# Attention steps between single matmuls, at distances of ScalarE's work, and feed-forward products opened by weight pieces

## The chip, the cores and the metric

One Trainium2 chip, eight NeuronCores. Each core runs the same program on two of the sixteen sequences; no core waits for another. The metric is the device time of the slowest core in microseconds. Before the change it is 1290.26 us (median of three runs, 1287.92 to 1292.53). A difference of 0.3%, about 4 us, is what such runs can tell from none.

A core has TensorE (matmuls into PSUM, 8 banks of 128 x 512 fp32), VectorE, ScalarE and GpSimd, and queues that start DMAs; most DMAs here go through SyncE's.

## The reference, cut to what matters

```
x = x + 0.5 * ffn(layernorm(x))       # layer 0
x = x + attention(layernorm(x))       # layer 1: 16 heads of 64, causal, 2048 positions
x = x + 0.5 * ffn(layernorm(x))       # layer 2, same weights as layer 0

ffn(z):   s = softmax(z @ W_gate)                 # 7 columns
          w = two largest of s, scaled to sum 1
          out = z @ W_shared.T + (w1 + w2 as dispatched) * (z @ W_expert.T) + bias
attention(z): q, k, v = z @ W.T + b; softmax(q k^T / 8, causal) v; @ Wp.T + bp
```

Every token keeps both of its expert shares and all experts have one matrix, so a feed-forward layer is one product with `W_shared + W_expert` and the gate a factor per token.

## The kernel before, in words

Tokens are handled in 32 tiles of 128, four of them to a chunk, so 8 chunks, four for each sequence. Matrices lie in SBUF as bf16. A **product** (kinds `f`, `q`, `k`, `v`, `p` in the order) is eight matmuls of 128 x 512 that add up in one PSUM bank (L982, L995, L1005, L1037). VectorE then reads the bank out (L1110, L1125, L1136, L1176). There are 384 products.

Attention goes by **quads** (`qd`): 320 of them, each for two heads and two blocks of 128 keys against the 512 queries of a chunk. On TensorE a quad k is `scores(k)` (4 matmuls, L899, into banks 0 to 3) and `values(k-2)` (8 matmuls, L922, into bank 4, and 4 that sum the exponentials, L930, into bank 5). ScalarE takes the exponentials of quad k (L1273, two instructions). On a diagonal block VectorE masks (`mk`, L1161). A **unit** is all quads of two heads and one chunk: 64 units of 2, 4, 6 or 8 quads. At its end (`oe`) VectorE copies bank 4 to `OS` (L1169) and bank 5 to `DSB` (L1170); TensorE spreads the sums over the partitions with one matmul (`bc`, L1026), ScalarE takes their logarithm and its exponential (L1282, L1284), GpSimd multiplies (L757), a DMA stores (`os`).

The order of all this is one list, `ORDER`, made before the program is built; **each engine walks the same list from its start to its end and issues its own share of each entry**. So an entry that waits on an engine holds back all behind it on that engine. `a_order` gives the start, q, k, v and layer 0's feed-forward; `c_order` gives projection and layer 2's feed-forward. `make_order` walks both and puts quads in: a running sum of (quads left) / (products left) lets 0, 1 or 2 quads follow each product. Of the 384 products 262 are followed by one quad, 30 by two, 92 by none (most of these at either end). `bc` stands after the product that follows its `oe`, ahead of the next quad.

`SHARED` gives each product and each small PSUM result (`t`, `ga`, `n`, `b2`, `bc`, `bb`) a bank in turn, in the order of the list. During attention there are **two such banks, 6 and 7**:

```
    if _e == ("qd", 0):
        EARLY = list(_uses)
        _banks = (6, 7)
```

`bank_free` makes TensorE wait until the bank's last result was read out, before it writes the first matmul of a new one:

```
                b, m = SHARED[en]
                if m:
                    e.wait_ge(r_sh[b], m)
```

At the start, the 16 pieces of the two feed-forward matrices (512 KB each, fp32, half h of the outputs by quarter m of the inputs) come by SyncE's queue, and `ws` j adds a pair into `WF` (VectorE, two of them on GpSimd, L660). A product `f` of layer 0, half h waits until all four sums of that half are done.

## Time and profile before

| | us |
|---|---|
| median of the runs | 1290.26 |
| the profiled execution | 1291.16 |
| span of its slowest core (core 3) | 1289.5 |
| spans of all eight cores | 1275.2 to 1289.5 |
| TensorE busy | 1163.5 (90%) |
| VectorE busy | 755.4 (59%) |
| ScalarE busy | 741.3 (57%) |
| GpSimd busy | 437.7 (34%) |

The span runs from the first to the last instruction of a core. Busy time of TensorE is the union of the matmuls' modelled durations, so a matmul's row is longer than the distance to the next one's start; distances between starts are the better price. In an entry of the timeline the brackets hold the idle time of the engine before it and who ended that.

### The profile page before, as it was taken

To read this page: it belongs to the slowest core of one execution; us is meant where nothing else is said; L and a number is where in the kernel's file an instruction comes from. 1 tells how busy PE (TensorE), PEld (TensorE's weight loads), DVE (VectorE), ACT (ScalarE), POOL (GpSimd) and SP (SyncE) were. 2 spreads that over 40 slices of the span, in tenths; PEclk is the share of its full clock that TensorE was granted. 3 is DMA by queue.
4 is the path that set the end of the run, shared out by engine and by line. 5 is a ranking of instruction groups with operands and counts; after the bars stand their busy time and mean duration, and the time that the engine had idled before them with its cause. 6 is when DMAs were issued, how large, how long until landed. Compare 5 with 4: busy or idle time off the path is not lost.

```text
span 1289.5 us, 28541 instructions; the slowest of 8 cores (1275.2 to 1289.5 us)
## 1 busy us (share of the span) xinstructions
PE 1163.5 (90%) x9038; PEld 436.5 (34%) x9038; DVE 755.4 (59%) x1366; ACT 741.3 (57%) x936; POOL 437.7 (34%) x310
## 2 busy tenths in 40 slices
PE   3789878899999999999999999998999999898987
PEld 1334333333333333333333333332333333333343
DVE  6774797557557555445645654545756555555575
ACT  4362243377577666667666676665666666665501
POOL 3422443136035113403511523621443260515152
PEclk9899999899999999999999999999999999999999
DMA  9979645697376437424634745645574754647052
GB/s 274 314 243 272 160 114 150 171 207 203 86 187 191 103 117 215 107 90 150 190 88 126 174 127 143 198 119 155 116 221 109 235 140 151 173 142 199 14 176 82
DMA packets 209350, 207.44 MB, mean 161 GB/s; under 512 B 127283, under 2 KB 172339, under 8 KB 209206
## 3 DMA queue, kind: packets, MB, share of 16 engines
q1 hardware_dynamic: 202304, 202.42, 57.0%
q10 hardware_dynamic: 6902, 3.20, 1.0%
q8 instruction: 78, 1.28, 0.5%
q14 instruction: 66, 0.54, 0.2%
HBM read 117.49 MB, written 67.11 MB: 143 GB/s over the span
## 4 chain that ended last, share of the span: by engine, by line
PE 65%; DVE 11%; ACT 8%; issue 7%; DMA 4%; SPq 4%; DVEq 0%; POOL 0%; ACTq 0%; POOLq 0%
PE PS L995 14%; PE PS L982 12%; PE PS L922 10%; PE PS L899 9%; PE PS L1005 8%; PE PS L1037 6%; ACT PT L1273 4%; PE PS L930 4%; ACT ATT L1273 3%; DVE PT L1161 2%; SPq L787 2%; DVE BNS L1054 2%; DMA WQKV<-od 2%; DMA WQKV<-wte 1%; DVE DSB L1170 1%
## 5 line engine op out<-in xcount | busy, mean ns | idle before, releaser
L1273 ACT ACTIVATE PT<-PS,MB 128x1024 bf16<-128x1024 f32 (+3 forms) x428 | 400.8, 989 | 224.0 <-PE PS L899 221.8
L982 PE MATMUL PS<-WF,XT 128*128 128x512 bf16 x1024 | 247.8, 392 | 10.0 <-DVE WF L660 8.5
L995 PE MATMUL PS<-XT,WQKV 128*128 128x512 bf16 x1024 | 247.0, 389 | 8.3 <-ACT XT L1207 3.1
L1273 ACT ACTIVATE ATT<-PS,MB 128x1024 bf16<-128x1024 f32 x212 | 193.8, 965 | 81.5 <-PE PS L899 80.7
L750 POOL TENSOR_TENSOR SQ<-QKS 128x512 bf16<-128x512 bf16 x128 | 140.8, 1102 | 277.4 <-DVE QKS L1125 227.0
L899 PE MATMUL PS<-ATT 64*128 64x512 bf16 (+3 forms) x1280 | 187.8, 351 | 39.6 <-ACT PT L1273 26.5
L757 POOL TENSOR_TENSOR OTT<-OS,RR 128x512 bf16<-128x512 f32 x64 | 83.2, 1301 | 411.1 <-ACT RR L1284 411.0
L982 PEld LDWEIGHTS PS<-WF,XT 128*128 128x128 bf16 x1024 | 95.1, 100 | 149.3 <-issue 56.5
L995 PEld LDWEIGHTS PS<-XT,WQKV 128*128 128x128 bf16 x1024 | 93.3, 99 | 146.8 <-issue 54.7
L732 POOL TENSOR_TENSOR XC<-XC,BF 128x1024 f32<-128x1024 f32 x48 | 104.4, 2176 | 95.2 <-DVE XN L1083 95.2
L1110 DVE SCALAR_TENSOR_TENSOR XC<-PS,GG,XC 128x512 f32<-128x512 f32 x96 | 71.7, 749 | 100.1 <-PE PS L982 98.2
L922 PE MATMUL PS<-PT,ATT 128*32 128x512 bf16 (+3 forms) x1712 | 120.4, 358 | 8.3 <-DVE PT L1161 8.2
L1005 PE MATMUL PS<-WQKV,XT 128*128 128x512 bf16 x512 | 120.1, 380 | 4.1 <-DVE VST L1136 2.5
L1054 DVE BATCH_NORM_STATS2 BNS<-XC 128x6 f32<-128x512 f32 x156 | 104.5, 688 | 17.4 <-DMA XC<-x 8.3
L899 PEld LDWEIGHTS PS<-ATT 64*128 64x128 bf16 x1280 | 46.5, 94 | 183.5 <-issue 183.3
L1125 DVE TENSOR_SCALAR QKS<-PS,BQ 128x512 bf16<-128x512 f32 x64 | 47.9, 749 | 83.4 <-PE PS L995 83.0
L1083 DVE TENSOR_SCALAR XN<-XC,MV,RS 128x1024 bf16<-128x1024 f32 x76 | 88.4, 1163 | 4.7 <-DMA XT<-XN 4.4
L1282 ACT ACTIVATE RR<-PS 128x512 f32<-128x512 f32 x64 | 38.2, 598 | 86.2 <-PE PS L1026 86.2
L1125 DVE TENSOR_SCALAR QKS<-PS,BK 128x512 bf16<-128x512 f32 x64 | 47.9, 749 | 61.3 <-PE PS L995 56.9
L1136 DVE TENSOR_TENSOR VST<-PS,BV 128x512 bf16<-128x512 f32 x64 | 44.1, 690 | 66.6 <-PE PS L1005 66.4
L930 PE MATMUL PS<-PT,ONES 128*32 128x512 bf16 (+3 forms) x856 | 82.6, 353 | 0.0
L1005 PEld LDWEIGHTS PS<-WQKV,XT 128*128 128x128 bf16 x512 | 45.8, 98 | 67.3 <-issue 20.0
(104 smaller groups left out, 1067.5 us busy)
## 6 DMA issues: line engine op xcount, KB each, us to landing
XC<-x SPq DMA_DIRECT2D x30, 512.0 KB, 7.5
x1d<-XC SPq DMA_DIRECT2D x30, 512.0 KB, 4.6
XC<-x1d SPq DMA_DIRECT2D x18, 512.0 KB, 6.6
out<-XC SPq DMA_DIRECT2D x18, 512.0 KB, 4.7
ATT<-qd SPq DMA_DIRECT2D x64, 128.0 KB, 3.4
od<-OTT SPq DMA_DIRECT2D x64, 128.0 KB, 2.4
ATT<-kd SPq DMA_DIRECT2D x16, 512.0 KB, 5.1
ATT<-vd SPq DMA_DIRECT2D x16, 512.0 KB, 5.9
```

The lines of the kernel that those rows point to most:

```text
L732: e.tensor_tensor(x, x, BF[:, :], ALU.add).then_inc(g_b[l], 1)
L750: e.tensor_tensor(SQ[:, m % 8, :], q, q, ALU.mult).then_inc(g_sq, 1)
L899: i = e.matmul(PS[:, S_BANK + 2 * m + h, off:512], kk[64 * h:64 * h + 64, (j + m) * 128:(j + m + 1) * 128], q[64 * h:64 * h + 64, off:512] ...
L922: e.matmul(PS[32 * g:32 * g + 32, O_BANK, off:512], vv[:, v + 32 * g:v + 32 * g + 32], ptile(k)[:, 2 * m + g // 2, off:512], start=(j + m ...
L930: i = e.matmul(PS[32 * g:32 * g + 32, D_BANK, off:512], ONES[:, 0:32], ptile(k)[:, 2 * m + h, off:512], start=(j == 0 and (m == 0 or c > 0 ...
L982: m = e.matmul(sbank(en), x[:, dc, t * 128:(t + 1) * 128], WF[:, dc, h * 512:(h + 1) * 512], start=(dc == 0), stop=(dc == DCN - 1))
L995: m = e.matmul(sbank(en), WQKV[:, int(w), dc, hp * 128:(hp + 1) * 128], XT2[:, i % 2, dc, :], start=(dc == 0), stop=(dc == DCN - 1))
L1005: m = e.matmul(sbank(en), XT2[:, i % 2, dc, t * 128:(t + 1) * 128], WQKV[:, 2, dc, h * 512:(h + 1) * 512], start=(dc == 0), stop=(dc == DC ...
L1054: m = e.bn_stats(BNS[:, b, 6 * h:6 * h + 6], xtile(l, n)[:, h * 512:(h + 1) * 512])
L1083: e.tensor_scalar(xn, xtile(l, n), MV[:, l, i % 2, t, 0:1], RS[:, l, i % 2, t:t + 1], ALU.subtract, ALU.mult).then_inc(v_a[l], 1)
L1125: was_read(e.tensor_scalar(QKS[:, m % NQK, :], sbank(en), bias[:, hp:hp + 1], None, ALU.add), en)
L1273: e.activation(ptile(k)[:, 2 * m:2 * m + 2, off:512], PS[:, S_BANK + 2 * m:S_BANK + 2 * m + 2, off:512], AF.Exp, bias=MB[:, u // HPN, hp % ...
```

## The change

1. `make_order`: a quad may now stand inside a product. The new entry `("pt", product, m)` means: issue the product's matmuls up to m, and leave the bank open. The planner counts TensorE's time since the last quad (`elapsed`, 213 ns a matmul, `tensor_work` for the quad) and starts the next when it reaches `need`, which is ScalarE's work on the quad (`scalar_work`) times the largest ratio of TensorE's to ScalarE's work over the chunks still to come. A quad may stand ahead of matmul 0, 2, 3, 4, 5 or 6 of a product.
2. `bc` may stand inside a product too: once `elapsed` is 2400 ns or more, or the next quad is due. `os` follows two products later.
3. `oe` copies `DSB` first and signals it by itself (`v_ds`), and `bc` waits for that.
4. At the start: the first four `f` of half 0 are issued as matmuls 0 to 3, 4 to 5 and 6 to 7 for the four tiles in turn, between the sums; the same for half 1, with half 0 of tiles 4 to 7 ahead of them; the broadcasts `bb` of two biases come later; `ws` 6 and 7 come behind `gb` and behind half 0 of tiles 4 to 7.
5. The host lays the two feed-forward matrices out by piece, so that a piece is 4 KB in one run for each partition and not two runs of 2 KB.

`SHARED` numbers a product at its first part; the banks stay 6 and 7. All products go through one function, `product(en, upto)`.

```
@@ -115,10 +115,12 @@
         o += [("a", 0, n), ("xf", 0, n), ("t", 0, n)]
     ws(1)
     o.append(("ga", 0, 0))
+    o += [("pt", ("f", 0, n, 0), 4) for n in range(4)]
     ws(2)
+    o += [("pt", ("f", 0, n, 0), 6) for n in range(4)]
     o.append(("gb", 0, 0))
     ws(3)
-    o += [("br", 1), ("br", 2)] + [("bb", r, h) for r in (1, 2) for h in range(2)]
+    o += [("br", 1), ("br", 2)]
     for n in range(4):
         o += [("st", n + 4), ("rt", 0, n + 4), ("a", 0, n + 4)]
         if n:
@@ -128,10 +130,12 @@
     ws(5)
     o += [("xf", 0, 5), ("f", 0, 3, 0), ("t", 0, 4), ("t", 0, 5), ("xf", 0, 6), ("t", 0, 6), ("xf", 0, 7), ("t", 0, 7)]
     o += [("s1", n, 0) for n in range(4)] + [("ga", 0, 1)]
+    o += [("bb", r, h) for r in (1, 2) for h in range(2)]
+    o += [("gb", 0, 1)] + [("f", 0, n, 0) for n in range(4, 8)]
+    o += [("pt", ("f", 0, n, 1), 4) for n in range(4)]
     ws(6)
-    o += [("gb", 0, 1), ("f", 0, 4, 0), ("f", 0, 5, 0)]
+    o += [("pt", ("f", 0, n, 1), 6) for n in range(4)]
     ws(7)
-    o += [("f", 0, 6, 0), ("f", 0, 7, 0)]
     for n in range(4):
         o += [("f", 0, n, 1), ("s1", n, 1), ("rt", 1, n)]
         one_cast()
@@ -282,31 +286,42 @@
 HEAVY = ("q", "k", "v", "f", "p")
+def step_cols(k):
+    c, j = QUADS[k][1], QUADS[k][3]
+    return [512 - k_off(c, j + m) for m in range(2)]
+def scalar_work(k):
+    w = sum(250 + 1.68 * n for n in step_cols(k)) if k < NQUAD else 0
+    return w + 1230 * is_end(k - LAG)
+def tensor_work(k):
+    n = sum(step_cols(k)) if k < NQUAD else 0
+    return 360 + 1.04 * n
+MATMUL = 213
+NDC = 8
 def make_order():
     other = a_order() + c_order()
     out = []
...
+    k = avail = before = loaded = 0
+    stored = set()
     def loads():
...
+        nonlocal loaded
+        while loaded < NUNIT and START[loaded + 1] <= avail and START[PRED[loaded] + 1] <= max(0, k - LAG):
+            out.append(("al", loaded))
+            loaded += 1
     heavy = [e[0] in HEAVY for e in other]
     first = other.index(("v", 3, 1))
@@ -316,43 +331,91 @@
         left -= heavy[end]
         end -= 1
     total = sum(heavy[first + 1:end + 1])
+    ready = [sum(heavy[first + 1:other.index(("v", 4 * i + 3, 1)) + 1]) + 6 for i in range(NCHUNK)]
+    elapsed = need = 0
+    ends, stores = [], []
     p = hold = wait = pend = 0
...
+    def step():
+        nonlocal k, elapsed, need
+        out.append(("qd", k))
+        v = k - LAG
+        if is_end(v):
+            out.append(("oe", QUADS[v][4]))
+            ends.append(QUADS[v][4])
+        if is_diag(k - 1):
+            out.append(("mk", k - 1))
+        elapsed = tensor_work(k) + min(max(0, elapsed - need), 500)
+        need = 2500
+        if k < NQUAD:
+            slow = 0
+            for i in range(QUADS[k][4] // HPN, NCHUNK):
+                until = ready[i + 1] if i + 1 < NCHUNK else total
+                todo = range(k, START[HPN * (i + 1)])
+                ahead = max(1, until - p) * NDC * MATMUL + sum(tensor_work(q) for q in todo)
+                slow = max(slow, ahead / sum(scalar_work(q) for q in todo))
+            need = scalar_work(k) * slow
+        k += 1
+        loads()
+    def spread():
+        u = ends.pop(0)
+        out.append(("bc", u))
+        stores.append([u, 2])
     for n, e in enumerate(other):
         if e[0] == "ol":
...
+            while HPN * e[1] + HPN - 1 not in stored:
+                if ends:
+                    spread()
+                elif stores:
+                    u = stores.pop(0)[0]
+                    out.append(("os", u))
+                    stored.add(u)
+                else:
+                    step()
+        if e[0] == "pt" or not heavy[n]:
+            out.append(e)
+            continue
+        if n > first:
             p += 1
             hold -= 1
             wait -= 1
             if wait == 0:
...
+                avail = pend
                 loads()
...
+            part = used = 0
+            for m in range(NDC):
+                if m not in (1, NDC - 1):
+                    due = elapsed >= need and (NQUAD <= k < NQUAD + LAG or k < avail and (hold < 0 or k < before))
+                    if ends and not used and (elapsed >= 2400 or due):
+                        if m > part:
+                            out.append(("pt", e, m))
+                            part = m
+                        spread()
+                        used = m > 0
+                    if due and not ends:
+                        if m > part:
+                            out.append(("pt", e, m))
+                            part = m
+                        step()
+                elapsed += MATMUL
+        out.append(e)
+        for s in stores:
+            s[1] -= 1
+        while stores and stores[0][1] <= 0:
+            u = stores.pop(0)[0]
+            out.append(("os", u))
+            stored.add(u)
+        if e[0] == "v" and e[1] % 4 == 3 and e[2] == 1:
+            pend, wait = START[HPN * (e[1] // 4) + HPN], 2 if e[1] > 3 else 5
+            hold, before = wait + 4, START[HPN * (e[1] // 4)]
+    while ends or stores:
+        if ends:
+            spread()
+        out.append(("os", stores.pop(0)[0]))
     return out
@@ -373,12 +436,14 @@
 for _e in ORDER:
+    if _e[0] == "pt":
+        _e = _e[1]
-    if _e[0] in ("bb", "t", "ga", "f", "q", "k", "v", "n", "b2", "bc", "p") and not by_dma(_e):
+    if _e[0] in ("bb", "t", "ga", "f", "q", "k", "v", "n", "b2", "bc", "p") and not by_dma(_e) and _e not in SHARED:
...
@@ -933,6 +997,52 @@
                                      stop=(j + m >= end - (1 if c else 0)))
                 i.then_inc(p_pv, 1)
+            done = {}
+            def product(en, upto):
+                kind = en[0]
+                begin = done.get(en, 0)
+                done[en] = upto
+                if not begin:
+                    bank_free(en)
...
+                for dc in range(begin, upto):
+                    if kind == "f":
+                        if en[1] == 0 and n == 0 and dc % 2 == 0:
+                            summed(e, 4 * h + dc // 2)
+                        a = xt(2 * en[1], i)[:, dc, t * 128:(t + 1) * 128]
+                        b = WF[:, dc, h * 512:(h + 1) * 512]
...
+                    m = e.matmul(sbank(en), a, b, start=(dc == 0), stop=(dc == DCN - 1))
+                if upto == DCN:
+                    was_filled(m, en)
             for en in ORDER:
                 kind = en[0]
                 if kind == "qd":
...
@@ -1166,8 +1234,8 @@
-                    e.tensor_copy(OS[:, u % 2, :], PS[:, O_BANK, :])
-                    e.tensor_copy(DSB[:, u % 2, :], PS[:, D_BANK, :]).then_inc(v_oe, 1)
+                    e.tensor_copy(DSB[:, u % 2, :], PS[:, D_BANK, :]).then_inc(v_ds, 1)
+                    e.tensor_copy(OS[:, u % 2, :], PS[:, O_BANK, :]).then_inc(v_oe, 1)
@@ -1311,6 +1379,9 @@
+    for k in ("wts", "wte"):
+        wT[k] = np.ascontiguousarray(wT[k].reshape(4, 2, 128, 2, 512).transpose(3, 0, 2, 1, 4).reshape(2, 4, 128, D))
```

## Rows read from the trace of the kernel before

**Rows 1.** The page: busy time, share of the span and instructions of each engine.

```profile
PE 1163.5 (90%) x9038; PEld 436.5 (34%) x9038; DVE 755.4 (59%) x1366; ACT 741.3 (57%) x936; POOL 437.7 (34%) x310
```

**Rows 2.** Windows: stretch, length, busy by engine (instructions), PEclk, DMA share, GB/s.

```profile
143.00:245.00 102.00, 80.83 (x566) 32.47 (x563) 77.88 (x148) 36.66 (x68) 36.03 (x25) 0.93 0.61 151
245.00:870.00 625.00, 594.92 (x4879) 214.00 (x4877) 342.54 (x644) 420.25 (x507) 205.53 (x159) 0.99 0.56 149
870.00:1215.00 345.00, 317.11 (x2619) 112.01 (x2620) 196.94 (x348) 221.21 (x257) 118.55 (x61) 0.98 0.56 154
```

**Rows 3.** Groups of TensorE, 245 to 1215 us: busy, mean ns, idle before.

```profile
L995 PE MATMUL PS<-XT,WQKV 128*128 128x512 bf16 x768 | 184.8, 384 | 1.4 <-DVE QKS L1125 0.7 <-DVE NQN L1141 0.3
L899 PE MATMUL PS<-ATT 64*128 64x512 bf16 (+3 forms) x1204 | 178.0, 353 | 37.7 <-ACT PT L1273 24.6 <-ACT ATT L1273 11.5
...
L922 PE MATMUL PS<-PT,ATT 128*32 128x512 bf16 (+3 forms) x1608 | 113.6, 359 | 5.4 <-DVE PT L1161 5.3
...
L1026 PE MATMUL PS<-DSB,SEL 128*128 128x512 bf16 x56 | 21.1, 377 | 6.9 <-DVE DSB L1170 6.1 <-DVE GD L1090 0.7
```

**Rows 4.** Timeline at 558 us: two quads in a row.

```profile
558.26 4.12 ACT L1273 ACTIVATE PT<-PS,MB 128x1024 bf16<-128x1024 f32 x4
...
559.50 0.39 PE L899 MATMUL PS<-ATT 64*128 64x512 bf16 x2 [1.32 <-ACT PT L1273]
...
560.51 0.60 PE L899 MATMUL PS<-ATT 64*128 64x512 bf16 x2 [0.61 <-ACT PT L1273]
```

**Rows 5.** Timeline at 460 us: quad, product, quad, read-out.

```profile
459.46 0.61 PE L899 MATMUL PS<-ATT 64*128 64x512 bf16 x4
...
460.70 1.90 PE L982 MATMUL PS<-WF,XT 128*128 128x512 bf16 x8
...
462.53 0.61 PE L899 MATMUL PS<-ATT 64*128 64x512 bf16 x4
462.78 0.75 DVE L1110 SCALAR_TENSOR_TENSOR XC<-PS,GG,XC 128x512 f32<-128x512 f32 x1 [1.14 <-PE PS L982]
```

**Rows 6.** Timeline at 204 to 210 us: one small result between two products.

```profile
204.29 1.90 PE L982 MATMUL PS<-WF,XT 128*128 128x512 bf16 x8
...
206.44 0.38 PE L1026 MATMUL PS<-DSB,SEL 128*128 128x512 bf16 x1 [0.25 <-DVE DSB L1170]
...
207.50 1.89 PE L1005 MATMUL PS<-WQKV,XT 128*128 128x512 bf16 x8 [0.69 <-DVE XC L1110]
...
209.23 0.22 PE L1021 MATMUL PS<-DG,ONES 128*128 128x128 bf16 x1
209.50 0.69 DVE L1136 TENSOR_TENSOR VST<-PS,BV 128x512 bf16<-128x512 f32 x1 [1.03 <-PE PS L1005]
...
210.34 3.61 PE L982 MATMUL PS<-WF,XT 128*128 128x512 bf16 x16 [0.89 <-DVE VST L1136]
```

**Rows 7.** Timeline at 463 us: end of a unit, VectorE's copies, the next read-out.

```profile
463.25 0.28 PE L930 MATMUL PS<-ATT,ONES 128*32 128x256 bf16 x4
...
464.66 0.69 DVE L1169 COPY OS<-PS 128x512 f32<-128x512 f32 x1
465.27 0.68 DVE L1170 CAST DSB<-PS 128x512 bf16<-128x512 f32 x1
465.87 0.74 DVE L1110 SCALAR_TENSOR_TENSOR XC<-PS,GG,XC 128x512 f32<-128x512 f32 x1
```

**Rows 8.** Timeline of the start, 29 to 61 us.

```profile
29.52 9.71 PE L982 MATMUL PS<-WF,XT 128*128 128x512 bf16 x32 [1.36 <-DVE WF L660]
...
55.64 1.22 DVE L660 TENSOR_TENSOR WF<-ATT 128x1024 bf16<-128x1024 f32 x1
...
57.22 5.20 PE L982 MATMUL PS<-WF,XT 128*128 128x512 bf16 x12 [7.12 <-DVE WF L660]
...
60.97 0.75 DVE L1110 SCALAR_TENSOR_TENSOR XC<-PS,GG,XC 128x512 f32<-128x512 f32 x1 [2.79 <-PE PS L982]
```

**Rows 9.** Windows: 10 to 50 us, while the feed-forward pieces come.

```profile
10.00:50.00 40.00, 26.44 (x196) 14.12 (x196) 32.70 (x56) 18.98 (x40) 19.52 (x9) 1.00 1.01 313
```

More of the change, by code:

```diff
@@ L318, in make_order @@
     total = sum(heavy[first + 1:end + 1])
+    ready = [sum(heavy[first + 1:other.index(("v", 4 * i + 3, 1)) + 1]) + 6 for i in range(NCHUNK)]
+    elapsed = need = 0
+    ends, stores = [], []
     p = hold = wait = pend = 0
-    late = []
-    def flush():
-        nonlocal late
-        out.extend(late)
-        late = [("os", e[1]) for e in late if e[0] == "bc"]
+    def step():
[23 more added lines that the diff above has]
+        stores.append([u, 2])
     for n, e in enumerate(other):
         if e[0] == "ol":
-            while ("os", HPN * e[1] + HPN - 1) not in out:
-                if not late:
-                    late = step()
-                flush()
-        out.append(e)
-        if e[0] in HEAVY:
-            flush()
-        if e[0] == "v" and e[1] % 4 == 3 and e[2] == 1:
-            pend, wait = START[HPN * (e[1] // 4) + HPN], 2 if e[1] > 3 else 5
-            hold, state["before"] = wait + 4, START[HPN * (e[1] // 4)]
-        if n > first and heavy[n]:
+            while HPN * e[1] + HPN - 1 not in stored:
[11 more added lines that the diff above has]
+        if n > first:
             p += 1
@@ L597, in build_program @@
         v_oe = sem("v_oevac")
+        v_ds = sem("v_sums")
         v_dg = sem("v_diag")
@@ L943, in tensor_program @@
                         values(k - LAG)
+                elif kind == "pt":
+                    product(en[1], en[2])
+                elif kind in HEAVY:
+                    product(en, DCN)
                 elif kind == "t" and en not in TDMA:
@@ L1024, in tensor_program @@
                     bank_free(en)
-                    e.wait_ge(v_oe, u + 1)
+                    e.wait_ge(v_ds, u + 1)
                     was_filled(e.matmul(sbank(en), SEL[:, 0 if u // HPN % 4 else 1, :], DSB[:, u % 2, :],
                                         start=True, stop=True), en)
-                elif kind == "p":
-                    n, h = en[1], en[2]
-                    i, t = divmod(n, 4)
-                    if t == 0 and h == 0:
-                        e.wait_ge(d_ol[i % 2], 16 * (i // 2 + 1))
-                    if n == 0 and h == 0:
-                        e.wait_ge(a_wc, 32)
-                    bank_free(en)
-                    for hp in range(HPN):
-                        m = e.matmul(sbank(en), otc(i)[:, hp, t * 128:(t + 1) * 128],
-                                     WP[:, hp, h * 512:(h + 1) * 512], start=(hp == 0), stop=(hp == HPN - 1))
-                    was_filled(m, en)
         def vector_program(e):
```

98 lines of the change are left out of this document (31 added, 67 removed).

## The prediction, made before the changed kernel was run

> **What bounds the kernel now.** I read the page first: TensorE is busy for 1163.5 of 1289.5 us, no other engine for more than 59% [rows 1]. TensorE's work sets the end, so what counts is what it loses between matmuls. The windows then say where: from 143 to 245 us it is busy for 80.8 of 102 us beside a VectorE busy for 77.9; from 245 to 1215 us for 594.9 + 317.1 = 912.0 of 970 us, which leaves 58 us idle [rows 2]. The groups of that stretch say why: the scores waited for ScalarE's exponentials for 24.6 + 11.5 = 36.1 us, the values for masks some 8 us (5.3 and a smaller group), `bc` for 6.9 us; products waited for almost nothing (1.4 us on the largest group) [rows 3]. The timeline shows the first of these: of two quads in a row the second waits 1.32 + 0.61 us, since ScalarE takes 1.03 us an exponential [rows 4]. With one quad per product the pattern is tight: quad 460.70 - 459.46 = 1.24 us, product 462.53 - 460.70 = 1.83 us, no wait [rows 5].
>
> The profiled execution took 1291.16 us, 0.9 us over the median; I sum against it and don't convert.
>
> **Part 1, distances by ScalarE's work.** A full quad has `scalar_work` 2 x (250 + 1.68 x 512) = 2220 ns; the ratio is about 1.3 (products left 314 x 8 x 0.213 = 535 us and quads 405 us, over ScalarE's 707 us, gives 1.33; it falls to 1.27). So `need` is about 2820, a quad sets `elapsed` to 1425, and the next follows after 6 or 7 matmuls: by the timeline's prices 1.24 + 6.5 x 0.22 = 2.7 us, against 2.06 us of exponentials plus a start 0.5 us late. ScalarE just fits. Two quads side by side without a product part are gone. Of the 36.1 us I take 33 as saved (bounds 20 and 36). The mask waits may shrink; I leave them, bounds -6 and +4. The granted clock was 0.99 for 625 us and 0.98 for 345 us [rows 2], a loss of 6.3 + 6.9 = 13 us; TensorE stood still 1 to 2 us before such slow stretches at the doubled quads. I take 6 back, bounds 0 and 12. The number of quads and products is as before, so switching between them costs what it did.
>
> **Part 2, `bc` inside a product.** This is where I expect the loss. Banks 6 and 7 are given out in turn. Before: product X in bank 6, `bc` in 7, a quad, product Y in 6. VectorE reads X out meanwhile: it starts 0.25 us after TensorE has gone on and takes 0.75 us (462.53, 462.78) [rows 5], so bank 6 is free about 1.05 us after X's last matmul, and `bc` with the quad covers 0.3 + 1.24 us. Now `bc` is issued at `elapsed` 2400, which is (2400 - 1425)/213, 5 matmuls after the quad that ended the unit; this quad's distance carries 1230 ns more, need (2220 + 1230) x 1.27 = 4380, so the next quad comes 14 matmuls after it, 9 after `bc`. X has at most 6 matmuls left after `bc`. So X ends, Y begins **in X's bank with nothing between**, and TensorE waits for the whole read-out. The trace has this wait even with a small matmul between: 0.69 us at 207.50 (product, `bc`, product) and 0.89 us at 210.34 (product, one matmul, product) [rows 6]. With nothing between I take 1.0 us.
>
> How often: I carried the distances through all 64 units by the rule. In 39 `bc` falls ahead of matmul 2 to 6 and neither a quad nor another small result comes before Y. In 13 it falls ahead of matmul 0: then X itself lies in the bank of the product before, with `bc` alone between, as at 207.50; 0.8 us. The rest are shifted by a gate, a norm or a due quad. 39 x 1.0 + 13 x 0.8 = 49 us (bounds 15, if VectorE is often early and others fill in, and 65).
>
> A second wait stands ahead of `bc`. Its bank is that of product W before X. Where the quad stood near W's end, VectorE's list is: `oe` (two copies, 0.61 us apart: 464.66, 465.27, 465.87), and only then W's read-out [rows 7]; W is read out 0.25 + 1.2 + 0.75 + 0.07 = 2.3 us after the quad, and `bc` comes 1.1 us after it. In 22 units the quad stands ahead of W's matmul 4 to 6 and `bc` ahead of X's 2 to 5: 22 x 1.2 = 26 us; in 5 more about 0.7, 4 us. Against these 30 us go the present `bc` waits of 6.9 us [rows 3], which part 3 (`DSB` first, 0.61 us earlier) largely removes: net +24 (bounds 0 and 35). Behind the waiting `bc` on TensorE stand the rest of X, Y and the next quad, so each of these microseconds is the whole core's; ScalarE, GpSimd and the stores wait with them and have slack.
>
> Ordinary products lose margin as well. Before, X's bank was wanted again after quad, product, quad, 1.24 + 1.83 + 1.24 = 4.3 us; now after one product with at most one quad inside, 1.7 to 3.1 us. VectorE is busy for 342.5 + 196.9 of 970 us [rows 2], so mostly in time; bounds 0 and +25. I take 3.
>
> Where the Trainium skill bears on this: a copy of a product out of PSUM runs beside the next product's matmuls in our rows, at 462.78 beside the quad [rows 5]. The Trainium skill (TensorE: Matmul & The Clock Gate, "Loop structure matters more than you think") says of such a copy that the next iteration's matmuls follow at once and the engine stays warm. By that rule alone the 49 + 24 us would not be there and the sum below would be 1244; the rows at 207.50 and 210.34 speak against it where both products share a bank.
>
> **Part 4, the start.** Before, half 1 of the first products began at 57.22, 7.12 us idle, behind the last sum at 55.64, and its first 12 matmuls came 0.43 us apart [rows 8]. That sum stood on VectorE behind the gate's small operations and two read-outs. Now half 0 of tiles 4 to 7 goes first, six of eight matmuls of the four half-1 products fill the idle time, and the last sum can follow at about 52.5: DMA moved 313 GB/s at a full share [rows 9], which brings the 4.2 MB of x and 8.4 MB of pieces in about 12.6/0.313 + 2 = 42 us plus what queues between, so by 50 us. The first half-1 read-out moves from 60.97 [rows 8] to about 55. After it VectorE's chain per tile (read-out, statistics, apply) sets the pace as before, so 6 us reach the start of attention. Half 0 also begins earlier than 29.52, but waits for x behind it: 1 of these 6. The wider runs of the pieces and the later `bb` (four matmuls, about 1 us) cancel. Take -6, bounds -11 and -1. Past the queues: SyncE's loads that wait for a sum's slot go with the sums, the last four earlier by 4 us and two later by 1 to 2 us.
>
> **143 to 245 us.** The 16 quads of the first chunk are spread over 27 products instead of 15, away from where VectorE is full [rows 2]. That should win some of the 21 us idle, and the eight units' `bc` waits (counted above) take it back. Take -2, bounds -10 and +6.
>
> **Sum:** -33 - 6 + 49 + 24 + 3 - 6 - 2 = +29; I leave 3 us for units of the first chunks whose waits lie under VectorE's: 1291.2 + 26 = **1317 us**.
>
> **The rivals.**
> - *The read-out waits stay small and the ScalarE waits go* (chance 0.25, with what lies between it and no change). For it: products waited 1.4 us in all of 768 matmuls [rows 3]; VectorE has room. Against: this rests on the 1.5 us between X and Y, which the new place of `bc` removes. Without any of it 1291.2 - 33 - 6 - 6 - 2 = 1244 us; with a third of the 73 us, 1268.
> - *Gains and waits cancel*, within 0.3% (0.09): 45 us of the 73; 1291.
> - *VectorE becomes late for ordinary products too* (0.12): with 1.7 us of margin each late read-out stops TensorE; at the upper bounds +25 and +65 the end is 1291 + 64 = 1350. For it: bursts of statistics, apply and copies of 2 to 3 us; against: 43% idle.
> - *The start's gain doesn't arrive* (an independent 0.2): DMA at a share of 1.01 [rows 9] delivers weights no sooner; +5 on any of these.
>
> The forecast has 0.54. Its own range is 1300 to 1340. From 1257 to 1345 the range takes in the larger part of the first rival and leaves out some 0.1 on each side. Faster by over 0.3% (4 us, what this measurement can tell): 0.25; within: 0.09; slower: 0.66.
>
> **What would show it.** Between 245 us and the end of attention: scores' waits for ScalarE under 8 us of 36.1; products' groups (L1044 or where the function puts them) with 45 to 60 us idle put down to VectorE's read-outs, in steps of 1 us, one for each unit; `bc` with 25 to 35 us idle put down to a read-out and not to `DSB`; granted clock nearer 1.00; first half-1 read-out near 55 us and the first quad near 137 instead of 143. Wrong if products wait under 15 us: then the order leaves something between X and Y that I missed. Wrong in size if idle time over attention stays at 58 us with other names.

## The result and the profile after: 1386.99 us, 7.5% slower

The changed kernel takes 1386.99 us (median of four runs, 1385.78 to 1388.09) against 1290.26 us for the kernel before on the same chip. The ratio is 1.075, with a 95% interval of 1.0723 to 1.0776. In some executions of any of these kernels the cores of one die show a lower granted clock than the others and take longer; every median and ratio here leaves those executions out. The prediction had the sign and not the size: 1317 us, range 1257 to 1345. The profiled execution has a span of 1385.2 us on its slowest core (core 5), 95.7 us more than before.

The page after, same first line as [rows 1]:

```profile
PE 1185.2 (86%) x9038; PEld 426.1 (31%) x9038; DVE 745.0 (54%) x1366; ACT 748.4 (54%) x936; POOL 446.1 (32%) x310
```

TensorE's idle time (span less busy) went from 1289.5 - 1163.5 = 126.0 us to 1385.2 - 1185.2 = 200.0 us, and the same 9038 matmuls were busy for 21.7 us longer. These 74.0 + 21.7 us are the whole of the 95.7. The windows, columns as in [rows 2], show the attention stretch, which now ends near 1300 us and not 1215:

```profile
143.00:245.00 102.00, 78.09 (x523) 28.65 (x522) 67.40 (x134) 34.26 (x64) 34.64 (x22) 0.87 0.55 127
245.00:930.00 685.00, 598.24 (x4811) 203.09 (x4811) 343.86 (x644) 417.38 (x499) 206.81 (x157) 0.99 0.49 135
930.00:1300.00 370.00, 324.01 (x2628) 110.75 (x2626) 192.66 (x347) 225.37 (x260) 124.87 (x64) 0.96 0.53 149
```

No engine got fuller; all wait more. From 143 to 245 us even fewer matmuls were done (523, before 566), at a granted clock of 0.87, before 0.93. Which waits, the groups of TensorE over the whole span tell (busy and mean ns, then idle before them and who ended it), the answer to [rows 3]. All products are now on one line, L1042:

```profile
L1042 PE MATMUL PS<-WF,XT 128*128 128x512 bf16 x1024 | 257.9, 395 | 14.1 <-DVE XC L1178 10.5 <-DVE WQKV L1178 2.8 <-DVE VST L1204 0.4
L1042 PE MATMUL PS<-XT,WQKV 128*128 128x512 bf16 x1024 | 256.7, 390 | 30.5 <-DVE QKS L1193 17.9 <-DVE XC L1178 6.2 <-ACT XT L1275 2.9
L963 PE MATMUL PS<-ATT 64*128 64x512 bf16 (+3 forms) x1280 | 178.8, 353 | 1.7 <-ACT PT L1341 1.1 <-ACT ATT L1341 0.2
L1042 PE MATMUL PS<-WQKV,XT 128*128 128x512 bf16 x512 | 129.9, 389 | 16.2 <-DVE VST L1204 11.0 <-DVE XC L1178 2.4 <-DVE QKS L1193 2.0
...
L1042 PE MATMUL PS<-WP,WQKV 128*128 128x512 bf16 x256 | 63.4, 385 | 12.3 <-DMA WQKV<-od 7.6 <-DVE XC L1244 2.0 <-DVE WQKV L1244 1.5
...
L1106 PE MATMUL PS<-DSB,SEL 128*128 128x512 bf16 x64 | 25.1, 393 | 56.1 <-DVE QKS L1193 20.8 <-DVE XC L1178 13.1 <-DVE DSB L1237 10.0
```

The same groups of the kernel before, over its whole span ([rows 3] has them from 245 to 1215 us only):

```profile
L982 PE MATMUL PS<-WF,XT 128*128 128x512 bf16 x1024 | 247.8, 392 | 10.0 <-DVE WF L660 8.5 <-DVE VST L1136 1.5
L995 PE MATMUL PS<-XT,WQKV 128*128 128x512 bf16 x1024 | 247.0, 389 | 8.3 <-ACT XT L1207 3.1 <-ACT WQKV L1226 2.0 <-DVE QKS L1125 1.8
L899 PE MATMUL PS<-ATT 64*128 64x512 bf16 (+3 forms) x1280 | 187.8, 351 | 39.6 <-ACT PT L1273 26.5 <-ACT ATT L1273 11.5
...
L1005 PE MATMUL PS<-WQKV,XT 128*128 128x512 bf16 x512 | 120.1, 380 | 4.1 <-DVE VST L1136 2.5 <-ACT WQKV L1226 0.9 <-DVE XC L1110 0.7
...
L1037 PE MATMUL PS<-WP,WQKV 128*128 128x512 bf16 x256 | 61.0, 385 | 4.2 <-DMA WQKV<-od 4.2
...
L1026 PE MATMUL PS<-DSB,SEL 128*128 128x512 bf16 x64 | 24.1, 377 | 12.8 <-DVE DSB L1170 9.0 <-DVE GD L1090 2.4 <-DVE NQN L1141 1.2
```

The scores wait 1.7 us, before 39.6: the gain is there. But the product groups wait 77.2 us in all (14.1 + 30.5 + 16.2 + 12.3 and 4.1 of a small group), before 26.6, and 61 us of that for VectorE's read-outs, before 6.5 (by the releasers that each group's line names). `bc` waits 56.1 us, before 12.8. The small results (transposes, gates, norm sums) wait 16 us more (38.1, before 22.0), the masked values 4 us more.

One wait of each kind in the timeline of the changed kernel (start, duration, then the idle time before it and its releaser). First the one predicted, `bc` inside a product and then a product in the bank just left:

```profile
600.87 0.68 DVE L1238 COPY OS<-PS 128x512 f32<-128x512 f32 x1
...
601.10 0.38 PE L1106 MATMUL PS<-DSB,SEL 128*128 128x512 bf16 x1
...
601.31 1.02 PE L1042 MATMUL PS<-WF,XT 128*128 128x512 bf16 x4
...
602.51 0.75 DVE L1178 SCALAR_TENSOR_TENSOR XC<-PS,GG,XC 128x512 f32<-128x512 f32 x1 [0.96 <-PE PS L1042]
...
603.41 1.24 PE L1042 MATMUL PS<-WF,XT 128*128 128x512 bf16 x5 [1.07 <-DVE XC L1178]
```

The product's part ends at 601.31 + 1.02 = 602.33; VectorE was free and read out from 602.51 to 603.26, and TensorE still lost 1.07 us. The two parts of one product around `bc`, and the product that waits, are all in bank 7. Then a wait ahead of `bc`: its bank is that of the product whose read-out (755.09) stood behind a mask:

```profile
754.89 0.28 DVE L1229 TENSOR_TENSOR PT<-PT,TRI 128x256 bf16<-128x256 bf16 x1
755.09 0.74 DVE L1193 TENSOR_SCALAR QKS<-PS,BQ 128x512 bf16<-128x512 f32 x1
...
756.09 0.38 PE L1106 MATMUL PS<-DSB,SEL 128*128 128x512 bf16 x1 [1.04 <-DVE QKS L1193]
```

The order of the list and the trace can be laid side by side, matmul by matmul. Between the first and the last quad 307 products (306 in e9) begin behind another product. They are sorted here by what TensorE does between the two: a quad or none, and whether the new product takes the bank that the product before has just left. The rows e3 to e12 are kernels of the experiments below.

| places: with a wait for VectorE, us in all | no quad between, same bank | no quad between, other bank | a quad between |
|---|---|---|---|
| before | 3: 2, 1.6 | 13: 2, 2.5 | 291: 7, 3.5 |
| changed kernel | 66: 64, 61.5 | 168: 1, 1.6 | 73: 1, 0.5 |
| e3 (`bc` passes its bank on) | 26: 17, 8.1 | 208: 0, 0.0 | 73: 1, 0.5 |
| e9 (`bc` between products) | 23: 21, 19.3 | 163: 2, 2.6 | 120: 7, 6.0 |
| e11 (doubles split) | 3: 2, 2.2 | 13: 2, 2.5 | 291: 9, 8.2 |
| e12 (all quads inside) | 84: 83, 73.4 | 214: 2, 2.5 | 9: 0, 0.0 |

So product next to product costs next to nothing as long as the second has the other bank; what waits is a product that wants the bank just left, with no quad in between. It is the same for `bc`. In 34 of the 64 units of the changed kernel no quad stands between the end of the product that had `bc`'s bank and `bc`; all 34 waited for VectorE, 45.1 us in all. In the other 30 none waited for a read-out, and 15 waited for `DSB`, 10.0 us. Before, 57 of 64 had a quad between, and none of these waited for a read-out. In e9 most `bc` have a whole product in that place and no quad: 19 of 62 waited for VectorE, 12.9 us.

### The profile page after: what moved, and what is told of

It reads as the page before. It is cut to its first block, busy times and chain, and to the rows that moved or that the text cites. A ratio compares the mean times of both kernels' runs of the same rounds, so it can differ in the third digit from the quotient of the medians.

```text
span 1385.2 us, 28550 instructions; the slowest of 8 cores (1372.0 to 1385.2 us)
## 1 busy us (share of the span) xinstructions
PE 1185.2 (86%) x9038; PEld 426.1 (31%) x9038; DVE 745.0 (54%) x1366; ACT 748.4 (54%) x936; POOL 446.1 (32%) x310
## 4 chain that ended last, share of the span: by engine, by line
PE 67%; DVE 15%; issue 9%; DMA 3%; ACT 2%; SPq 1%; DVEq 1%; POOL 1%; ACTq 0%; POOLq 0%
PE PS L1042 41%; PE PS L986 10%; PE PS L963 10%; PE PS L994 4%; DVE QKS L1193 2%; DVE BNS L1122 2%; DVE XC L1178 2%; PE PS L1106 1%; DVE DSB L1237 1%; DVE VST L1204 1%; DVE PT L1229 1%; DVE OS L1238 1%; DMA ATT<-wte 1%; DMA WQKV<-od 1%; DVE XN L1151 1%
## 5 line engine op out<-in xcount | busy, mean ns | idle before, releaser
L1042 PE MATMUL PS<-XT,WQKV 128*128 128x512 bf16 x1024 | 256.7, 390 | 30.5 <-DVE QKS L1193 17.9
L1042 PE MATMUL PS<-WF,XT 128*128 128x512 bf16 x1024 | 257.9, 395 | 14.1 <-DVE XC L1178 10.5
L816 POOL TENSOR_TENSOR SQ<-QKS 128x512 bf16<-128x512 bf16 x128 | 147.7, 1157 | 278.3 <-DVE QKS L1193 235.0
L963 PE MATMUL PS<-ATT 64*128 64x512 bf16 (+3 forms) x1280 | 178.8, 353 | 1.7 <-ACT PT L1341 1.1
L1042 PEld LDWEIGHTS PS<-XT,WQKV 128*128 128x128 bf16 x1024 | 90.9, 99 | 173.2 <-issue 90.7
L1042 PE MATMUL PS<-WQKV,XT 128*128 128x512 bf16 x512 | 129.9, 389 | 16.2 <-DVE VST L1204 11.0
L1042 PEld LDWEIGHTS PS<-WF,XT 128*128 128x128 bf16 x1024 | 93.5, 100 | 155.2 <-issue 69.5
L1151 DVE TENSOR_SCALAR XN<-XC,MV,RS 128x1024 bf16<-128x1024 f32 x76 | 80.6, 1060 | 5.9 <-DMA XT<-XN 4.8
L1229 DVE TENSOR_TENSOR PT<-PT,TRI 128x256 bf16<-128x256 bf16 x162 | 72.1, 483 | 8.6 <-ACT PT L1341 8.0
```

What stands on the lines that cost most here:

```text
L816: e.tensor_tensor(SQ[:, m % 8, :], q, q, ALU.mult).then_inc(g_sq, 1)
L963: i = e.matmul(PS[:, S_BANK + 2 * m + h, off:512], kk[64 * h:64 * h + 64, (j + m) * 128:(j + m + 1) * 128], q[64 * h:64 * h + 64, off:512] ...
L1042: m = e.matmul(sbank(en), a, b, start=(dc == 0), stop=(dc == DCN - 1))
L1151: e.tensor_scalar(xn, xtile(l, n), MV[:, l, i % 2, t, 0:1], RS[:, l, i % 2, t:t + 1], ALU.subtract, ALU.mult).then_inc(v_a[l], 1)
L1229: e.tensor_tensor(p, p, TRI[:, :].unsqueeze(1).broadcast_to([128, 2, 128]), ALU.mult).then_inc(v_mk, 1)
```

## The experiments

"Planner" below is `make_order`, "start order" the head of `a_order`. Ratios are against the kernel before on the same chip. Lines shown are TensorE's groups over the whole span unless said otherwise.

### Which part costs

**e1_start_only**: changed kernel, `make_order` of before.

> The changed kernel with the planner of before, so only the start, the weights laid out by piece and the sums copied first are new. Theory: the first scores come 3.3 us earlier in the changed trace (140.3 against 143.6 us), and all of the loss lies behind them, so this runs in 1285 to 1289 us, 2 to 6 under before. Rival: the new start or the new layout costs something later (DMA, VectorE), then it is at or over 1292.

Measured: 1280.8 us, ratio 0.994 (0.9919 to 0.9968), some 4 us under the theory's range. **e2_planner_only**: changed kernel, start order of before.

> The changed kernel with the start order of before. Theory: the planner alone makes the loss of 96 us, so 1388 to 1393 us. Rival: start and planner work against each other (the later start shifts the first chunks), then it differs from 1387 by over 10 us.

Measured: 1378.7 us, 1.070 (1.0669 to 1.0734), under the theory's 1388 and 8 us from the changed kernel, so neither theory nor rival by its number. Still the new planner costs by itself more than the whole loss (103 us over e7 below, which is e2 without it), and the new start order, put on top, costs 8 where the theory had it gain. To part the rest: **e8_layout_only**, the kernel before with the pieces laid out in 4 KB runs:

```
-  src = (wts, wte)[j % 2].rearrange(...)[:, 2*m:2*m+2, h*512:(h+1)*512]
+  src = (wts, wte)[j % 2][h, m]
```

> The kernel before with the new layout of the two feed-forward matrices only (4 KB in one run for each partition). Theory: 8 us earlier at the start of attention, all else as before: 1280 to 1284 us. Rival: the layout does nothing and the early start came from the order of the sums or of the copies: 1288 to 1292.

Measured: 1285.0 us, 0.9976 (0.9956 to 0.9996), a gain of about 3 us by the ratio, less than the 8 us expected. **e7_cheap_parts**: that, with `DSB` copied first and `v_ds`, everything else of before.

> The kernel before with the two small parts only: weights laid out by piece, sums copied and signalled first. Old planner, old start order. Theory: with the old start order and the new layout attention began at 133.7 us in the median of the cores (142.0 before, 139.5 in the changed kernel, 140.8 with new start order and old planner), so the layout alone is worth 8 us and the new start order costs 6; the sums first are worth 7 in attention. So 1272 to 1278 us, under the 1281.4 of the start-only kernel. Rival: the early start is given back in the first chunks, where VectorE is full; then 1280 to 1285.

Measured: 1275.9 us, 0.990 (0.988 to 0.9914). The layout and `DSB` first give 1% together, and the start order takes some of it back: e1 is 5 us over e7, the changed kernel 8.3 over e2.

Why it takes it back, VectorE's rows tell. In the changed kernel the last half-1 sum stands behind the read-outs of half 0 of tiles 4 to 7. The gate's factor `GG` is there at 48.0; from then on each read-out waits for its own product, so the sum goes by TensorE's pace:

```profile
47.83 0.16 DVE L1172 TENSOR_REDUCE GG<-GW 128x4 f32<-128x8 f32 x1
...
51.19 0.75 DVE L1178 SCALAR_TENSOR_TENSOR XC<-PS,GG,XC 128x512 f32<-128x512 f32 x1 [1.95 <-PE PS L1042]
...
54.64 0.75 DVE L1178 SCALAR_TENSOR_TENSOR PT<-PS,GG,PT 128x512 f32<-128x512 f32 x1 [0.97 <-PE PS L1042]
...
56.44 1.22 DVE L726 TENSOR_TENSOR WF<-ATT 128x1024 bf16<-128x1024 f32 x1
```

In e2, with the old order and the new layout, the same sum is 5.5 us earlier:

```profile
50.90 1.22 DVE L722 TENSOR_TENSOR WF<-ATT 128x1024 bf16<-128x1024 f32 x1
```

The new start order also ran at a lower granted clock. From 10 to 50 us it was 0.83 to 0.87 on all eight cores, and 0.91 to 1.00 both before and in e2. On core 5 TensorE was busy for only 4.2 of the 10 us from 30 on, and from 40 to 48.5 us the granted clock was 0.50, its lower level of 1.2 GHz; before, on core 3, it was busy for all 10 and kept 1.00. The window of the changed kernel, against [rows 9]:

```profile
10.00:50.00 40.00, 24.50 (x177) 13.45 (x178) 32.22 (x60) 19.04 (x40) 23.16 (x10) 0.83 1.01 331
```

### Inside the planner: the bank and the place of `bc`

**e3_bank_passed_on**: `bc` takes its bank but does not advance the turn, so the next product has the bank of `bc` and not the one just left.

```
-        _turn += 1
+        _turn += _e[0] != "bc"
```

> The changed kernel, but a bc does not advance the turn of the two shared banks: the product after it takes the bc's own bank, which ScalarE has read by then, and not the bank of the product around it. Theory: the wait of the next product for the read-out of the one that held the bc is about 1.2 us in some 40 units, so 45 to 60 us go: 1327 to 1342 us. The waits ahead of bc (some 45 us) stay. Rival A: ordinary products have too little margin for VectorE anyway; then most waits only change their place and it stays over 1370. Rival B: splitting a product costs by itself in switching, then the product waits go and the time falls by under half of them.

Measured: 1346.9 us, 1.046 (1.0422 to 1.05): 40 us back, a few less than the theory's 45. The next product now waits for ScalarE to read `bc` out (`RR`), 18 us over all groups; `bc` itself waits as in the changed kernel:

```profile
L1042 PE MATMUL PS<-WF,XT 128*128 128x512 bf16 x1024 | 255.2, 393 | 5.4 <-ACT RR L1350 4.9 <-DVE VST L1204 0.4
L1106 PE MATMUL PS<-DSB,SEL 128*128 128x512 bf16 x64 | 25.3, 396 | 55.7 <-DVE QKS L1193 20.7 <-DVE XC L1178 13.1 <-DVE DSB L1237 9.5
```

**e4_bc_later**: `elapsed >= 2400` becomes 3700, six matmuls later.

> The changed kernel, but a bc is placed from 3700 ns of the planner's time on and not from 2400, so 11 matmuls after the quad that ended its unit, when VectorE has done both copies and the read-out of the product before. Theory: the waits ahead of bc (61 of them hold 77 us between the start of the matmul before and bc's own, of which about 63 us are waits) fall to under 15 us, the waits of the next product (about 50 us) stay: 1335 to 1350 us. Rival: the wait is for the sums' copy or for VectorE's load in general, then it follows bc to its new place and the time stays over 1370.

Measured: 1354.4 us, 1.051 (1.0473 to 1.0554): 33 us back, 4 us short of the theory. `bc` gives 24 of it, 56.1 to 32.1 us and not to under 15, and the slowest core's clock rose from 0.965 to 0.973; the products waited no less than in the changed kernel:

```profile
L1106 PE MATMUL PS<-DSB,SEL 128*128 128x512 bf16 x64 | 24.8, 388 | 32.1 <-DVE QKS L1193 10.1 <-DVE XC L1178 8.4 <-DVE XC L1244 5.1
```

**e5_bank_and_later**: both.

> The changed kernel with both edits: a bc doesn't advance the turn of the banks, and it comes from 3700 ns on. Each alone took 40 and 33 us off 1387. Theory (two separate waits, one ahead of bc, one of the next product): they add, 1305 to 1325 us. Rival (one delay of VectorE that shows in two places, or ScalarE's read-out of bc now in the way, with only 2 to 6 matmuls between bc and the product that takes its bank): they don't add, 1335 to 1350 us.

Measured: 1332.7 us, 1.035 (1.0324 to 1.0367): 54 us back, not the 73 of the sum, and between the ranges of theory and rival. The products' waits for ScalarE's read of `bc` grew from 18 us in e3 to 25, since `bc` later leaves less of the product between. Taken one at a time the edits gave 40 and 33 us. Neither wait is gone with both of them in: `bc` still waits 32.0 us, and the time is still 3.5% over the kernel before.

**e9_bc_at_boundary**: e2 with `bc` only between two products and right ahead of a quad; quads still go inside products.

```
-    if ends and not used and (elapsed >= 2400 or due):
-        if m > part: out.append(("pt", e, m)); part = m
+    can = NQUAD <= k < NQUAD + LAG or k < avail and (hold < 0 or k < before)
+    due = can and elapsed >= need - (850 if ends else 0)
+    if ends and m == 0 and (due or not can and elapsed >= 2400):
         spread()
```

> The changed planner and the old start order, but bc stands only ahead of a product's first matmul, with the next quad right behind it (up to 850 ns of planner's time early). Quads still stand inside products. Theory: then bc's bank and the next product's are both read out in time, so both waits go (100 us of them) while ScalarE is still not waited for: 1378.7 - 100 to 130 = 1250 to 1275 us. Rival: quads inside products cost by themselves (switching, lost margin of the read-outs); then it stays over 1290.

Measured: 1315.3 us, 1.020 (1.0187 to 1.0221): 63 us less than e2, far from the theory's 1275 and over the rival's 1290. `bc` has its margin again; the scores wait more (20.8 us, in the changed kernel 1.7), now that a quad is drawn up to 850 ns early for `bc`; and a DMA is late, the attention output that the projection loads (`od`), 12.6 us (4.2 before):

```profile
L956 PE MATMUL PS<-ATT 64*128 64x512 bf16 (+3 forms) x1280 | 186.5, 354 | 20.8 <-ACT PT L1334 13.8 <-ACT ATT L1334 6.1
L1099 PE MATMUL PS<-DSB,SEL 128*128 128x512 bf16 x64 | 24.9, 389 | 13.7 <-DVE QKS L1186 7.8 <-DVE XC L1171 2.7 <-DVE XC L1237 1.3
L1035 PE MATMUL PS<-WP,WQKV 128*128 128x512 bf16 x256 | 64.0, 393 | 13.1 <-DMA WQKV<-od 12.6 <-DVE XC L1237 0.2 <-DVE WQKV L1237 0.2
```

**e10_small_results**: e9, and a small result (`n`, `ga`, `b2`, a transpose) likewise draws the next quad ahead of the product that follows it, up to 850 ns early, so that no two products around it meet in one bank with nothing else between.

> The kernel with bc at a boundary ahead of a quad (1315.3 us), and the same for the small results n, ga, b2 that take a turn of the two banks: the quad after them is drawn to the boundary if it is due within 850 ns. Theory (same-bank waits behind small results): in that kernel the steps from a product to a small result and back held 43 us against 15 in the kernel with the old planner, so 12 to 25 us go: 1290 to 1303. Rival (VectorE's read-outs have too little margin once quads stand inside products, wherever the small results are): within 6 us of 1315.

Measured: 1.0196 (1.0143 to 1.0249), with runs at 1313.4 and 1316.8 us: no gain. The edit did what it was meant to at its places: products that want the bank just left, with no quad between, fell from 23 to 10, and their waits from 19.3 to 10.6 us. But the drawn quads made the scores wait 27.6 us, in e9 20.8. The waits behind small results are real; this way of removing them costs as much as they do.

**e13_readout_first**: e9, with VectorE's copies and mask of a quad that stands inside a product put behind that product's read-out.

```
-    out.append(("oe", QUADS[v][4]))
+    (behind if inside else out).append(("oe", QUADS[v][4]))
```

> The kernel with bc at a boundary (1315.3 us), and where a quad stands inside a product, VectorE's copies (oe) and masks (mk) of that quad stand behind the product's read-out in the list, not ahead of it. Theory: of the 65 us that are left against the kernel with split doubles (1250), a part is that read-outs wait behind two copies of 1.2 us together or masks of 0.9 us, with only one product of 1.7 us as margin: bc's waits (some 13 us) and products' waits on VectorE (some 29 us) halve, 1292 to 1303 us. Rival A: it is the spacing by itself that costs (ScalarE's waits of 20 us, late stores, masks); no change, 1311 to 1318. Rival B: late masks and copies now hold the values back: over 1320.

Measured: 1377.7 us, 1.070 (1.0666 to 1.0728), 62 us worse than e9, as rival B has it. The wait only changed its place: the values wait for masks that stand behind a read-out which itself waits for the product to end. The waits of e13, total, times, longest:

```profile
PE PS L985 <- DVE PT L1228: 45.5, 49, 3.2
...
PE PS L985 <- DVE ATT L1228: 18.8, 15, 2.9
```

### The position of a quad, with the list held fixed

All of these build on e7 (1275.9 us), whose planner is that of the kernel before, so the same quads follow the same products.

**e11_doubles_split**: where two quads would stand in a row, the second goes inside the next product, ahead of its matmul 4. `bc` stays between products.

```
+        if second and heavy[n]:
+            out.append(("pt", e, 4))
+            mid = step()
+            second = 0
         out.append(e)
```

> The kernel with the cheap parts (new layout, sums first, old planner and start: 1275.9 us), but where two quads followed one product, the second goes inside the next product, ahead of its matmul 4. All else of the order stays. Theory: the 29 steps from quad to quad held 27.8 us and the scores' waits for ScalarE some 37 us, most at these places; half of that goes and nothing comes for it, since a quad still stands behind nearly every product: 1248 to 1262 us. Rival: a split product costs as much in switching and in late read-outs as the wait it saves; then 1270 to 1280.

Measured: ratio 0.970 (0.9658 to 0.9738), with runs at 1248.8, 1251.0 and 1252.7 us. This beats both kernels: by their middle one it is 136 us under the change, 39 under before and 25 under e7. In e7 and e11 the scores' groups and `bc`:

```profile
L900 PE MATMUL PS<-ATT 64*128 64x512 bf16 (+3 forms) x1280 | 186.4, 351 | 40.6 <-ACT PT L1278 26.0 <-ACT ATT L1278 11.3 <-DMA ATT<-vd 1.7
...
L1043 PE MATMUL PS<-DSB,SEL 128*128 128x512 bf16 x64 | 24.5, 382 | 4.2 <-DVE GD L1095 1.6 <-DVE NQN L1146 1.2 <-DVE DSB L1174 0.6
```

```profile
L910 PE MATMUL PS<-ATT 64*128 64x512 bf16 (+3 forms) x1280 | 186.8, 350 | 18.5 <-ACT PT L1288 10.2 <-ACT ATT L1288 4.7 <-DMA ATT<-vd 1.2
...
L1053 PE MATMUL PS<-DSB,SEL 128*128 128x512 bf16 x64 | 24.4, 381 | 3.4 <-DVE NQN L1156 1.2 <-DVE GD L1105 0.7 <-DVE DSB L1184 0.6
```

22 us of ScalarE waits went, and nothing came in their place: products waited 21.5 us in all in e7 and 23.4 in e11. The mean granted clock of the slowest core rose from 0.982 to 0.990. The pattern, in e11's timeline, is product, quad, product, `bc`, quad, product:

```profile
562.62 1.90 PE L989 MATMUL PS<-WF,XT 128*128 128x512 bf16 x8
...
564.36 0.38 PE L1053 MATMUL PS<-DSB,SEL 128*128 128x512 bf16 x1
...
564.67 0.60 PE L910 MATMUL PS<-ATT 64*128 64x512 bf16 x4
564.70 0.75 DVE L1125 SCALAR_TENSOR_TENSOR XC<-PS,GG,XC 128x512 f32<-128x512 f32 x1
...
566.03 1.89 PE L989 MATMUL PS<-XT,WQKV 128*128 128x512 bf16 x8
```

VectorE reads the product's bank out from 564.70 while the quad holds TensorE, and the next product, in the same bank 7, starts at 566.03 with no wait.

**e12_all_inside**: the same list, but every quad moved to matmul 4 of the next product (where there were two, to 2 and 6), with nothing between two products but `bc` or a small result.

> The kernel with the cheap parts (1275.9 us), same quads after the same products, but each is moved by half a product, to matmul 4 of the next one (two at 2 and 6). The distances of quads are as in the old planner, so this changes only what stands between one product's end and the next one's start. Theory: with no quad there, a bc or small result between two products leaves the second in the first one's bank with about 0.3 us between: 62 bc x 1.1 us + 30 small results x 0.7 us, less up to 30 us of waits for ScalarE at the doubled quads: 1310 to 1345 us. Rival: the loss of the changed kernel comes from the new distances and not from where quads stand; then 1250 to 1285.

Measured: 1333.5 us, 1.035 (1.0296 to 1.0405), as the theory has it, so 58 us over e7 from position alone. Its waits:

```profile
PE PS L994 <- DVE QKS L1145: 33.7, 29, 4.9
PE PS L994 <- DVE VST L1156: 20.4, 29, 1.5
PE PS L994 <- DVE XC L1130: 13.3, 13, 1.5
```

and one of them in its timeline, product, `bc`, product, with VectorE's read-out behind two copies:

```profile
603.27 1.04 PE L994 MATMUL PS<-WF,XT 128*128 128x512 bf16 x4
...
604.21 0.68 DVE L1190 COPY OS<-PS 128x512 f32<-128x512 f32 x1
...
604.43 0.38 PE L1058 MATMUL PS<-DSB,SEL 128*128 128x512 bf16 x1
...
604.80 0.74 DVE L1130 SCALAR_TENSOR_TENSOR XC<-PS,GG,XC 128x512 f32<-128x512 f32 x1
...
606.27 1.02 PE L994 MATMUL PS<-XT,WQKV 128*128 128x512 bf16 x4 [1.46 <-DVE XC L1130]
```

The second product of each such pair wants the bank that the first has just left. This list has no new distances and no `bc` inside a product, and it waits in the same way: at 83 of the 84 places of that kind, and at 2 of the 214 where product follows product in the other bank. Product groups wait 87.0 us (e7: 21.5), `bc` 16.1 (4.2), the scores 7.3 (40.6): +65.5 + 11.9 - 33.3 = 44 of the 57 us between the two spans; the matmuls were busy for another 13.5 us.

**e14_best_readout_first**: e11 with the copies and masks of the 30 moved quads behind the product's read-out.

> The kernel with split doubles (1250 us), and the same turn of VectorE's work at its 29 quads inside products. Theory: in the old spacing a read-out has 4 us of margin, so nothing waits for it: 1247 to 1253 us. Rival: the masks and copies get late for the values: 1254 to 1262.

Measured: 1290.5 us, 1.002 (1.0008 to 1.0034), 40 us worse than e11 and far over both theory and rival. The values waited for masks for 24.2 + 8.5 us and, since bank 4 wasn't copied out in time, 13.9 us for `OS`; e13's result again, at 30 places. Copies and masks ahead of the read-out, as the changed kernel has them, is the right order.

## Why the prediction was right in sign and wrong in size

The mechanism was right: `bc` inside a product makes TensorE wait for read-outs. The steps that failed are three terms of the sum. The matmuls' own time was to fall by 6 us with the clock and rose by 22. The small results and masks were put at 0 ("switching between them costs what it did") and cost, with `od`, 23. The wait ahead of `bc` was put at +24 and measured +43.

*ScalarE's waits* (-33): right. The scores' idle time fell by 37.9 us (39.6 to 1.7).

*The product behind `bc`* (+49) *and ordinary margin* (+3): right together. The products' waits for VectorE's read-outs rose by 54 us. e3, which takes away the first kind and pays 18 us for it, gave 40 back. Count and price were right as well: 39 places with nothing between, 1.15 us each (1.0 taken), and 11 with `bc` alone between, 0.9 us each (13 and 0.8 taken). e3 and e12 together say what the reason is. It isn't `bc` inside a product: e12 has none and waits 73.4 us. Nor is it product next to product: e3 has 208 such places in the other bank and waits at none. It is that a product wants **the bank just left, and no quad stands between**.

*Ahead of `bc`* (+24): mis-sized. It measured 56.1 - 12.8 = +43 us, over my upper bound of 35. I counted 27 units, those in which `oe` stood ahead of the read-out, at 30 us. All 34 units without a quad between the bank's last product and `bc` waited, 45.1 us; VectorE's list has more in it than `oe`, a mask for one at 754.89, just ahead of the read-out at 755.09. And I took 6.9 us off, because `DSB` comes first. In e7 that wait does go (9.0 to 0.6 us), but in the changed kernel it is 10.0, since `bc` is wanted sooner behind the unit's last quad. I priced one queue pattern and left out what else VectorE's list holds.

*"Switching costs what it did"* and the masks' bound of +4 (0): wrong. Small results wait 16 us more, of which 8 are norm sums and `GG`'s spreading that wait for a product's read-out (a small result also takes a bank in turn, and the same quad is missing ahead of it) and 8 are transposes that wait for the normed tile `XN`; the values wait 4 more for masks, the projection 3.4 for `od`.

*The granted clock* (-6): wrong in sign. The slowest core's mean went from 0.979 to 0.965. Over the busy time that is 0.021 x 1163.5 = 24 us lost before and 0.035 x 1185.2 = 41 after, +17 and not -6. Part of it lies at the start (10 to 50 us: 0.83, and 1.00 before). I had seen that TensorE stood still before slow stretches at the doubled quads, and took the cure; I didn't ask what about a hundred new pauses of 1 us would do. It isn't the pauses' sum alone, though: e12 stands still for 163 us and its slowest core has 0.984, e9 for 143 us and 0.973. Which pauses lower the clock stays open.

*The start* (-6): -2.5 us reached the start of attention (142.0 to 139.5, median over cores, by the first scores), for other reasons than given. The layout, which I had cancelled against `bb`, brought the gain; my step "the last sum can follow at about 52.5" failed. It came at 56.44, and the first half-1 read-out at 60.25 and not near 55, since I read when the DMA would have the piece and not what stands ahead of the sum on VectorE: four read-outs, each of which waits for its product.

Against the idle time and the busy time of the page: read-outs ahead of products +54, `bc` +43, small results, masks and `od` +23, scores -38, weight sums at the start (`WF`, 8.5 before) -8, and matmuls busy for longer +22: 96, for the 95.7 us measured. I predicted +26: the read-outs and the scores right to 5 us each, and 19 us short on `bc`, 23 on the small things, and 28 on the matmuls' own time (-6 taken). The granted clock accounts for some 17 of these 22 us, by the estimate above.

The rivals: the one with 1350 us, VectorE late for ordinary products too, was nearest, and got 0.12. Its number was near by luck: the 241 products of the table that had the other bank or a quad in between waited for VectorE for 2.1 us in all. What the Trainium skill (TensorE: Matmul & The Clock Gate, "Loop structure matters more than you think") says of the copy out of PSUM, that it leaves the next iteration's matmuls to follow at once, holds in the changed kernel at 167 of the 168 places where no quad stands between and the next product has the other bank: no wait for VectorE. It does not hold at 603.41, where the next one has the same bank: 1.07 us.

**What stays open.** e9 has `bc` between products and quads inside, at the new distances, and is still 64 us over e11. Their spans differ by 68.8 us: 46 idle (143.3 and 97.3) and 22.8 busy. The products wait 24.6 us more (10.9 of it for `od`), `bc` 10.3, masks 4, norm sums 3.5, scores 2.3, and the clock of the slowest core is 0.973 against 0.990. More product next to product than in e11 is not the reason: by the table 163 such places in the other bank cost 2.6 us. The 23 places in the same bank cost 19.3 us, in e11 2.2. e10 took 9 us of these away and paid 7 at the scores, and e13 shows that another order of copies and read-outs is worse. No run removes the rest: the late `od`, the masks and the lower clock.

## What to carry to other kernels

With two PSUM banks in turn, what matters is what TensorE does between leaving a bank and wanting it again, and it has to cover the read-out and whatever stands ahead of it in the reader's list. A block of other work is worth most between two products that share a bank; between products in different banks it isn't needed. Before moving it, go through the list bank by bank and count what is left between one use and the next, for the small results as well. To even out work that comes in pairs, move only the second of the pair (e11: 2% over e7), and keep everything else where it is. Masks and copies that a later matmul waits for go ahead of a read-out that isn't yet ready (e13, e14).

## What the runs showed of the hardware

- **A bank given back costs 1.07 us even with an idle reader**: 0.18 us until VectorE starts (602.33 to 602.51), 0.75 to read, 0.15 until TensorE is back (603.41).
- **4 KB in one run for each partition against two runs of 2 KB** moves the first 40 us. The issue of the last half-1 piece on SyncE's queue, in the kernel before:

```profile
33.35 2.91 SPq L787 DMA_DIRECT2D ATT<-wte  x1
```

and in e8, where the same bytes are issued 9 us earlier:

```profile
24.20 1.23 SPq L786 DMA_DIRECT2D ATT<-wte  x1
```

From 10 to 50 us the DMAs moved 333 GB/s against the 313 of [rows 9]. The last half-1 sum came at 50.20 and not at 55.64. Of that, about 3 us (0.24%) reach the end. The Trainium skill (DMA: Bandwidth & Descriptors, "Specifications") gives 512 B as the least transfer for line rate; both layouts are above it and still not equal here.
- **The clock does not go by the sum of the pauses.** In 245 to 870 us the granted clock is 1.00 in e7, e11 and e12 alike, though e12 stands still there for 61 us and e11 for 19; e9 stands still for 46 us and has 0.98. From 143 to 245 us it falls from 0.95 in e7 to 0.90 in e12, and to 0.87 in the changed kernel. The window of e12:

```profile
143.00:245.00 102.00, 78.21 (x526) 29.26 (x526) 73.70 (x138) 32.46 (x60) 34.49 (x22) 0.90 0.53 131
245.00:870.00 625.00, 564.12 (x4585) 191.01 (x4581) 323.50 (x610) 399.17 (x476) 200.04 (x152) 1.00 0.52 141
```
